# A decoder layer: the attention output turned in 32x32 blocks on VectorE and moved by DMA, in place of TensorE's turn

## The reference

```
q, k, v = x @ Wq, x @ Wk, x @ Wv          # 16 heads of 128
q, k    = rmsnorm(q, q_rms_w), rmsnorm(k, k_rms_w)
scores  = q k^T / sqrt(128) - alibi slope * distance, causal
y       = rmsnorm(softmax(scores) v, subln_w)       # per head, over its 128 columns
x       = layernorm(x + y @ Wproj)                  # y: 1024 x 2048, Wproj: 2048 x 256
x       = layernorm(x + x mixed by softmax(query key^T), query and key from ctx)
x       = layernorm(x + quantised feed-forward(x))  # ternary weights, 8-bit activations
```

## Time and profile before

| | |
|---|---|
| median of 3 runs | 435.72 us (434.96 to 436.02) |
| span of the profiled execution, first to last instruction | 432.9 us |
| time of that execution apart from its span | not given; the median of the runs lies 2.82 us above the span |
| TensorE matmul busy | 401.9 us (93%) |
| VectorE busy | 327.7 us (76%) |
| ScalarE busy | 254.4 us (59%) |
| GpSimd busy | 220.2 us (51%) |
| mean granted TensorE clock | 0.979 |
| DMA | 14.52 MB, 21747 packets |

### The profile page before, as it was taken

One profiled execution on the slowest core, in us unless ns is written; L12 is line 12 of the kernel. 1 busy time (PEld: TensorE's weight loads), 2 busy tenths in 40 slices (PEclk: granted clock), 3 DMA queues, 4 the chain that ended last, 5 costly groups with the idle time before them and its releaser, 6 DMA issues.

```text
span 432.9 us, 9595 instructions
## 1 busy us (share of the span) xinstructions
PE 401.9 (93%) x2605; PEld 361.1 (83%) x2612; DVE 327.7 (76%) x1000; ACT 254.4 (59%) x750; POOL 220.2 (51%) x368
## 2 busy tenths in 40 slices
PE   4979999999999999999999999999999899999552
PEld 3668899999999999999999999999988677777321
DVE  0777987887797798788779779878822788888862
ACT  3486777677676776767767677676722333333321
POOL 3633667676675776767767677675501122222210
PEclk9999999999999999999999999999999999999965
DMA  8980010110101101011010110000000000000000
GB/s 223 316 251 2 2 36 3 38 37 0 36 0 36 36 0 36 0 36 36 0 36 0 36 36 0 0 0 0 0 2 0 2 0 15 12 14 12 13 14 24
DMA packets 21747, 14.52 MB, mean 34 GB/s; under 512 B 1760, under 2 KB 21472, under 8 KB 21728
## 3 DMA queue, kind: packets, MB, share of 16 engines
q1 hardware_dynamic: 21728, 14.29, 11.2%
HBM read 13.24 MB, written 1.05 MB: 33 GB/s over the span
## 4 chain that ended last, share of the span: by engine, by line
PE 86%; DVE 5%; ACT 4%; issue 2%; DMA 1%; POOL 1%; SPq 0%; POOLq 0%; DVEq 0%
PE ps L482 30%; PE ps L422 11%; PE ps L493 7%; PE ps L506 6%; PE ps L499 5%; PE ps L512 4%; PE ps L505 3%; PE ps L514 3%; PE ps L513 3%; PE ps L521 3%; PE ps L587 3%; PE ps L572 2%; ACT hT L696 2%; DMA x_sb<-in_x 1%; PE ps L557 1%
## 5 line engine op out<-in xcount | busy, mean ns | idle before, releaser
L315 POOL TENSOR_TENSOR qk_rstd<-qk_sum,minus_half 128x2 f32<-128x2 f32 x128 | 88.5, 692 | 92.6 <-DVE qk_sum L797 90.8
L482 PE MATMUL ps<-w_hi,xT_hi 128*128 128x384 f32 x256 | 96.9, 378 | 2.3 <-DVE qk_n L791 1.4
L482 PE MATMUL ps<-w_hi,xT_lo 128*128 128x384 f32 x256 | 86.5, 338 | 0.0
L482 PE MATMUL ps<-w_lo,xT_hi 128*128 128x384 f32 x256 | 86.3, 337 | 0.0
L797 DVE TENSOR_REDUCE qk_sum<-sq 128x2 f32<-128x258 f32 x128 | 53.6, 419 | 30.8 <-ACT sq L635 29.1
L635 ACT ACTIVATE sq<-ps 128x256 f32<-128x256 f32 x128 | 49.1, 384 | 34.6 <-PE ps L482 34.4
L791 DVE TENSOR_TENSOR qk_n<-ps,qk_rstd 128x256 f32<-128x256 f32 x128 | 54.2, 423 | 18.8 <-POOL qk_rstd L315 17.8
L422 PE MATMUL ps<-wp,yT 128*128 128x256 f32 x256 | 62.2, 382 | 0.0
L310 POOL TENSOR_TENSOR y_rstd<-y_sum,minus_half 128x2 f32<-128x2 f32 x64 | 49.0, 766 | 24.6 <-DVE y_sum L804 20.9
L673 ACT ACTIVATE sqy<-ps 128x258 f32<-128x258 f32 x64 | 24.8, 387 | 58.5 <-PE ps L514 58.5
L422 PEld LDWEIGHTS ps<-wp,yT 128*128 128x128 f32 x256 | 46.7, 190 | 5.9
(11 more groups left out here) (126 smaller groups left out, 846.9 us busy)
## 6 DMA issues: line engine op xcount, KB each, us to landing
w_raw<-in_L_attn_Wq SPq DMA_DIRECT2D x16, 128.0 KB, 2.2
w_raw<-in_L_attn_Wk SPq DMA_DIRECT2D x16, 128.0 KB, 2.3
w_raw<-in_L_attn_Wv SPq DMA_DIRECT2D x16, 128.0 KB, 2.3
wp<-in_L_attn_Wproj SPq DMA_DIRECT2D x1, 2048.0 KB, 16.1
ff_raw<-in_L_ffn_w_gate SPq DMA_DIRECT2D x1, 1024.0 KB, 8.6
ff_raw<-in_L_ffn_w_up SPq DMA_DIRECT2D x1, 1024.0 KB, 11.0
ff_raw<-in_L_ffn_w_down SPq DMA_DIRECT2D x1, 1024.0 KB, 13.0
out<-fin SPq DMA_DIRECT2D x8, 128.0 KB, 1.7
```

What stands on the lines that cost most here:

```text
L315: pool.tensor_tensor(qk_rstd[:, t, :], qk_sum[:, t, :], minus_half[:], ALU.pow).then_inc(s_rs[t], 1)
L482: last = pe.matmul(ps[:, t, 0:3 * D], xa[:, k, tok], wa[:, r, k * 3 * D:(k + 1) * 3 * D], start=(i == 0), stop=(i == len(parts) - 1))
```

## The change

VectorE turns y_n itself, in 32x32 blocks: an operation `turn_y` behind pT in the step writes all 4 x 4 blocks of both tiles, each turned, to a new buffer `y_blk`. A block is then on the wrong partitions still, except on the diagonal; SyncE moves the blocks by DMAs within SBUF into `yT`, 16 for each head, each 32 partitions by 1 KB. `y_blk` has two halves, for even and odd heads. Within `yT` a head's columns are now ordered so that the eight token tiles lie side by side: a tile's 128 columns have a stride of 8 elements (32 bytes), and the projection's stationary operand is read so. The last three steps (`LATE`) are still turned by TensorE and copied by ScalarE, after the DMAs of their head have landed.

`sub_scale` is no longer applied with the copy but multiplied into `wp`, in four operations on VectorE at the ends of steps 4 to 7. The early projections take 14 heads; heads 14 and 15 of the first two tiles follow behind the drain. Several small buffers of the last stage now lie in `y_blk`.

```diff
+            def move_y(h, r):
+                for db in range(4):
+                    for tb in range(4):
+                        sp.dma_start(yT_cols[db * Q:(db + 1) * Q, bass.ds(h * (B * T) + tb * Q * NT, Q * NT)],
+                                     y_blk[tb * Q:(tb + 1) * Q, r, db].rearrange("p q u -> p (q u)")
+                                     ).then_inc(s_ydma[r], 16)
...
+            with sp.Fori(2, TRIPS) as trip:
                 for r in range(2):
                     sp.wait_ge(s_split, trip * (2 * SPLITS) + SPLITS * (r - 1))
                     load_w(trip * 2 + r, r)
+                    sp.wait_ge(s_blk, trip * PAIR + (r - 3) * B)
+                    move_y(trip * 2 + (r - 4), r)
+            for h in range(H - 4, H):
+                sp.wait_ge(s_blk, h * B + (B if h < H - 1 else B - LATE))
+                move_y(h, h % 2)
...
-                    last = pe.matmul(ps[:, u % 2, 0:C], yT[:, h * B + b, t * P:(t + 1) * P], wp[:, h, :],
+                    last = pe.matmul(ps[:, u % 2, 0:C], yT_parts[:, h, :, u], wp[:, h, :],
...
-                if live(3):
+                if live(3) and isinstance(n, int) and n - 3 >= STEPS - LATE:
                     pe.wait_ge(s_yn, n - 2)
-                    wait(pe, s_yT, n - 3)
+                    wait(pe, s_yT, n - 3 - (STEPS - LATE))
                     for t in range(TT):
                         last = pe.transpose(ps_yT[:, t * P:(t + 1) * P], y_n[:, t, :], ident[:])
...
+            for u in range(TT):
+                project(u, [H - 2, H - 1])
...
-                if live(4):
-                    act.wait_ge(s_ty, n - 3)
-                    act.activation(yT[:, n - 4, :], ps_yT, ACT.Copy, scale=sub_scale).then_inc(s_yT, 1)
+                if isinstance(n, int) and n - 4 >= STEPS - LATE:
+                    act.wait_ge(s_ty, n - 3 - (STEPS - LATE))
+                    act.wait_ge(s_ydma[1], 256 * TRIPS)
+                    own = (n - 4) % B * TT
+                    act.copy(yT_parts[:, H - 1, :, own:own + TT].rearrange("p w t -> p t w"),
+                             ps_yT.rearrange("p (t w) -> p t w", t=TT)).then_inc(s_yT, 1)
...
+            def turn_y(n, j, trip):
+                r, b = j // B, j % B
+                dve.wait_ge(s_yn, n - 2)
+                if b == 0:
+                    wait(dve, s_ydma[r], trip * 256)
+                dve.transpose(y_blk[:, r, :, :, b * TT:(b + 1) * TT].rearrange("p g q t -> p t g q"),
+                              y_n[:].rearrange("p t (g q) -> p t g q", g=4)).then_inc(s_blk, 1)
+
+            def scale_wp(part):
+                dve.wait_ge(s_wp, 16)
+                dve.wait_ge(s_vecs, 3)
+                rows = wp[:, part * 4:(part + 1) * 4].rearrange("p h c -> p (h c)")
+                dve.tensor_scalar(rows, rows, sub_scale, None, ALU.mult).then_inc(s_wps, 1)
...
                     dve.tensor_copy(pT[:], ps_pT).then_inc(s_pT, 1)
+                if live(3) and not (isinstance(n, int) and n - 3 >= STEPS - LATE):
+                    turn_y(n, (j - 3) % PAIR, trip)
                 if live(0):
                     norm(0, n)
...
+                if isinstance(n, int) and B <= n < PAIR:
+                    scale_wp(n - B)
```

More of the change, by code:

```diff
@@ L55, in decoder_kernel @@
     TRIPS = H // 2
-    EARLY = -(-TT * H // 6)
+    Q = P // 4
+    LATE = 3
+    EARLY = -(-TT * (H - 2) // 6)
     CROSS_STEP = 3
@@ L83, in decoder_kernel @@
         yT = sb("yT", [P, STEPS, T])
+        y_blk = sb("y_blk", [P, 2, 4, Q, NT])
         ident = sb("ident", [P, P])
@@ L135, in decoder_kernel @@
         x2 = sb("x2", [P, 2, C])
-        fin = sb("fin", [P, 2, C])
-        x1T = sb("x1T", [P, KC, P])
+        spare_f32 = y_blk[:, 1].rearrange("p g q u -> p (g q u)")
+        fin = spare_f32[:, 0:2 * C].rearrange("p (a c) -> p a c", a=2)
+        x1T = spare_f32[:, 2 * C:3 * C].rearrange("p (k t) -> p k t", k=KC)
+        x_round = spare_f32[:, 3 * C:4 * C]
         x_most, x_scale, x_inv, h_most, h_scale, h_inv, down_scale = (sb(n, [P, 1]) for n in (
@@ L146, in decoder_kernel @@
         sig, hid, h_round = ff_raw[:, 0, 0:F], ff_raw[:, 0, F:2 * F], ff_raw[:, 1, 0:F]
-        hq = sb("hq", [P, F], BF16)
-        hT = sb("hT", [P, FC, P], BF16)
+        spare = y_blk[:, 0].rearrange("p g q u -> p (g q u)").bitcast(BF16)
+        hq = spare[:, 0:F]
+        hT = spare[:, F:2 * F].rearrange("p (f t) -> p f t", f=FC)
         ps = ctx.enter_context(nc.psum_tensor("ps", [P, 8, BANK], F32))
@@ L157, in decoder_kernel @@
         ps_yT = ps[:, 6, 0:T]
+        yT_cols = yT[:].rearrange("p n t -> p (n t)")
+        yT_parts = yT_cols.rearrange("p (h w u) -> p h w u", h=H, u=NT)
         s_x = [sem("x_batch0_loaded"), sem("x_other_batches_loaded")]
@@ L184, in decoder_kernel @@
             "pT_copied", "y_done", "y_squared", "y_summed", "y_normed", "y_turned", "yT_copied"))
+        s_blk = sem("y_blocks_turned")
+        s_ydma = [sem("y_even_head_moved"), sem("y_odd_head_moved")]
+        s_wps = sem("wp_scaled")
         s_mv = [sem(f"mean_var{i}_done") for i in range(3)]
@@ L245, in _ @@
             sp.dma_start(wp[:], wproj.rearrange("(h p) c -> p h c", p=P)).then_inc(s_wp, 16)
-            with sp.Fori(1, TRIPS) as trip:
+            def move_y(h, r):
[4 more added lines that the diff above has]
+                                     ).then_inc(s_ydma[r], 16)
+            for r in range(2):
+                sp.wait_ge(s_split, 2 * SPLITS + SPLITS * (r - 1))
+                load_w(2 + r, r)
+            with sp.Fori(2, TRIPS) as trip:
                 for r in range(2):
@@ L415, in project @@
                         if u < 2:
-                            pe.wait_ge(s_wp, 16)
+                            pe.wait_ge(s_wps, 4)
                             pe.wait_ge(s_qkn[u], STEPS)
+                            pe.wait_ge(s_ydma[0], 256 * (TRIPS - 1))
+                            pe.wait_ge(s_ydma[1], 256 * (TRIPS - 1))
                         else:
                             pe.wait_ge(s_mv[0], u - 1)
-                    if h in (0, H - 1):
-                        pe.wait_ge(s_yT, h * B + b + 1)
-                    last = pe.matmul(ps[:, u % 2, 0:C], yT[:, h * B + b, t * P:(t + 1) * P], wp[:, h, :],
+                    if h == H - 2 and u == 0:
+                        pe.wait_ge(s_ydma[0], 256 * TRIPS)
+                    if h == H - 1 and u == 0:
+                        pe.wait_ge(s_ydma[1], 256 * TRIPS)
+                    if h == H - 1 and b > B - LATE - 1 and t == 0:
+                        pe.wait_ge(s_yT, b - (B - LATE) + 1)
+                    last = pe.matmul(ps[:, u % 2, 0:C], yT_parts[:, h, :, u], wp[:, h, :],
                                      start=(h == 0), stop=(h == H - 1))
@@ L427, in project_early @@
             def project_early(part):
-                for i in range(part * EARLY, min((part + 1) * EARLY, TT * H)):
-                    project(i // H, [i % H])
+                for i in range(part * EARLY, min((part + 1) * EARLY, TT * (H - 2))):
+                    project(i // (H - 2), [i % (H - 2)])
             def beside(n):
@@ L547, in _ @@
                     if m == 0:
-                        pe.wait_ge(s_yT, STEPS)
+                        pe.wait_ge(s_yT, LATE)
                     for k in range(KC):
@@ L689, in _ @@
                     act.wait_ge(s_t1, m + 1)
-                    act.copy(x1T[:].rearrange("p k t -> p (k t)"), ps[:, 2, 0:C]).then_inc(s_x1T, 1)
+                    act.copy(x1T.rearrange("p k t -> p (k t)"), ps[:, 2, 0:C]).then_inc(s_x1T, 1)
                 if m > 0:
@@ L695, in _ @@
                     act.wait_ge(s_th, u + 1)
-                    act.copy(hT[:].rearrange("p f t -> p (f t)"), ps[:, 2, :].bitcast(BF16)).then_inc(s_hT, 1)
+                    act.copy(hT.rearrange("p f t -> p (f t)"), ps[:, 2, :].bitcast(BF16)).then_inc(s_hT, 1)
                 if m < NT:
@@ L810, in step @@
                     dve.wait_ge(s_ry, n - 2)
-                    wait(dve, s_ty, n - 3)
+                    if isinstance(n, int) and n - 3 > STEPS - LATE:
+                        dve.wait_ge(s_ty, n - 3 - (STEPS - LATE))
                     dve.tensor_tensor(y_n[:], ps_y[:, :, 0:D], y_rstd[:].unsqueeze(2).to_broadcast([P, TT, D]),
@@ L894, in _ @@
                     dve.wait_ge(s_hr, u + 1)
-                    dve.tensor_scalar(hq[:], h_round, ROUND + 127.0, -ROUND, ALU.min, ALU.add).then_inc(s_hq, 1)
+                    dve.tensor_scalar(hq, h_round, ROUND + 127.0, -ROUND, ALU.min, ALU.add).then_inc(s_hq, 1)
                 if m > 1:
@@ L901, in _ @@
                     link(act_scale(x_most[:], x_scale[:], x_inv[:]))
[L902 to L903 removed]
+                    link(dve.tensor_scalar(x_round, x2[:, m % 2], x_inv[:], ROUND, ALU.mult, ALU.add))
+                    dve.tensor_scalar(xq[:], x_round, ROUND + 127.0, -ROUND, ALU.min, ALU.add).then_inc(s_xq, 1)
                     dve.tensor_scalar(gate_up_scale[:], w_scale[:, 0:2], x_scale[:], None, ALU.mult).then_inc(s_gus, 1)
```

1 line of the change is left out of this document (removed).

## The result

The changed kernel takes 462.36 us (median, 461.27 to 463.19) against 435.34 in the same series: slower, ratio 1.061 (95% interval 1.059 to 1.064). The forecast was 451, so the sign held, and the size fell short by 11: 462 lies above the band that the forecast gave itself (443 to 460) and inside its wide range (440 to 468). The span of the profiled execution went from 432.9 to 460.2, +27.3 us, where the sum said +15.1.

The account below looks back on a forecast made before the run. The prediction took TensorE as the bound, with a VectorE-GpSimd ring close behind. Loop 10.8, first-trip turns 1.65, scaling 2.0 and moves 0.7 made +15.1 us, a span of 448.0 and a median of 451 (443 to 460; wide range 440 to 468).

Parts of the forecast that it names:

- the sum: Whole kernel: loop 10.8, first trip's turns 1.65, scaling 2.0 and final moves 0.7 add 15.1 us to the profiled span.
- the turn in the ring: Loop, VectorE between pT and tile 0's norm: the turn adds 0.42 us, lengthening seven trips by 10.8 us.
- the ring: Each step: VectorE's norms, sums and copies, then GpSimd's power, which releases the next qk_n; 4.67 us when quantising.
- TensorE is the bound by a few tenths: Loop: TensorE sets plain steps at 4.42 us, with 0.34 us of room before it would wait for qk_n.
- the removal: TensorE's two turns per step go in 61 of 64 steps, 0.23 us a pair, at most 14.0 us.
- The double turn of the rivals: VectorE's turn takes twice per column for its stride, 0.69 us, giving 467 us; chance 0.22.
- The first trip: Before the loop: the turn in five steps adds 1.65 us, the four Wproj scalings on VectorE 2.0 us.
- Strided weight loads at nothing: Projections: reading yT at a 32-byte stride costs nothing, since the 0.11 us load may double under a 0.24 pass.
- The rival on it: Projections: strided weight loads take three times 0.11 us, adding 25 us over 256 passes, giving 476; chance 0.08.
- the prediction's own signs of being wrong: Wrong if TensorE stays without idle time in the loop, or if the passes after the loop lengthen.
- The moves at the end, 0.7: Drain: 32 DMAs for heads 14 and 15 land 17 us after step 59's turn, costing 0 to 2 us, taken as 0.7.
- The hidden turn of the other side: Loop: the turn falls wholly into VectorE's gaps and TensorE stays the bound, giving 424 us; chance 0.15.

Follow-up runs that it names:

- e7: The changed kernel without the call of turn_y, SyncE moving zeros; 442.55 us, 1.016 of the kernel before.
- e4: The changed kernel with the same strided turn put behind the scores, last in VectorE's step; 451.90 us, 1.040 of the kernel before.
- e5: The kernel before with VectorE's turn added behind pT, nothing taken out and nothing reading the turned blocks; 448.26 us, 1.029 of the kernel before.
- e3: The changed kernel with the turn writing 256 contiguous columns instead of columns 32 bytes apart; 454.43 us, 1.044 of the kernel before.
- e2: The changed kernel with the projection reading 128 contiguous columns of yT instead of strided ones; 458.77 us, 1.056 of the kernel before.
- e1: The changed kernel with heads 14 and 15 moved in four DMAs each instead of sixteen; 456.43 us, 1.050 of the kernel before.
- e8: The changed kernel with dense turn and read, the turn at two other places, head 15 kept on TensorE, head 14's passes last; 431.82 us, 0.992 of the kernel before.

## Why the prediction was right in sign and short in size

It was right in sign by its own mechanism, the turn in the ring. That 462 still falls into the wide range is partly luck: the range reached up to 468 for a turn of twice the price, which did not come; the drain and the strided loads, priced at 0.7 and 0, filled its place with 12.1.

- **TensorE is the bound by a few tenths, the ring stands close behind.** Right. e7 takes TensorE's work away and puts no turn in its place: four steps of a trip fall to between 4.20 and 4.29, close to the forecast 4.19 of TensorE's own work, which runs back to back there, and the three with quantising stay at 4.66 to 4.76, the ring's (the eighth, behind these, at about 4.39). That is what the removal is worth, 5.3 us of 14.0.
- **The turn in the ring.** The mechanism was right (e4, e5), the term mis-sized: the turn holds the next norm for 0.48, not 0.42. With 0.48 the forecast's sums give 4.47, 4.68 and 5.06, a trip of 38.16; measured were about 4.45, 4.66 and 5.01 to 5.10, 38.02. So the loop cost 12.8, not 10.8. Dense it would have been 0.36 (e3), below my 0.42, because a turn does overlap its neighbours, which I had denied it: it lasts 0.43 and the next operation starts after 0.36. What I priced from dense rows came out above it through the stride.
- **The double turn of the rivals.** Its cause was there, its price not: 0.63 busy against 0.43 dense, 0.48 against 0.36 start to start. By the Trainium skill (Advanced Engine Details and Errata, SBUF Cachelines), an access that goes to another 16-byte line each time is penalised. e2 and e3 agree in sign, and the penalty here is 1.3 to 1.5 times for the turn and 333 / 196 = 1.7 times for the weight load.
- **The first trip.** Too high by 1.3: the four scalings cost 1.30 (I took 2.0) and the five turns 0.98 (1.65), so part of each was hidden in that trip; where, I didn't follow.
- **Strided weight loads at nothing.** Wrong: 0.033 us a pass in a row, 3.3 us in the last stage (e2). "It may double under its cover" bounded the load against the pass of 0.24, by a row of a turn (0.11), which is a quarter of four matmuls on the chain and not a load (the page of before has 140 ns for those loads), and not by the projection's own load of 190 ns, which that page had too and which fills most of a pass, not a third; a load of 333 ns is longer than the pass. The rival on it had the mechanism and 25 us for it, against 3.3 in the last stage. Longer passes stood among the prediction's own signs of being wrong.
- **The moves at the end, 0.7.** This is the step that failed most: 8.85. Four terms of it were off. An issue took 0.64, not the 0.47 of a load. So the last block landed 343.56 - 321.66 = 21.9 us after the turn of step 59, not 17. And ScalarE stood at its copy already 13.5 us after it (343.56 - 8.37 - 321.66), where I had counted on about 17. The wait was 8.4 us, and with the lower clock behind it the passes took 2.1 more (e1). And the projections of heads 14 and 15, said only to change places, became the last thing that the first residual waits for, 3.34 us in e1, part of the remaining 2.4. I had followed the queue to its landing and stopped there, without timing the one who waits.
- **The hidden turn of the other side.** e8 shows that it can be had, by another place and a dense layout; but its price of 14.0 was the removal at face value, and with the turn wholly hidden it was 5.9 in the loop.

What stays open: which of the two new places in e8 brings more, how much of its gain is the place and how much the dense turn, and how the 2.4 us at the end of e1's drain divide between the late place of the projections and their stride; none of these was run alone.

## What to carry to other kernels

Work taken off the engine that bounds is worth only the distance to the ring behind it; read that distance step by step before pricing the removal. Work added to a second engine costs by its place in that engine's order: between a value and the engine that waits for it, it cost most of what it lasts (0.32 of 0.48 us a step here); in the time in which the engine itself waits, a third of that (e4), and dense and at the two places of e8 nothing. Where a change gives a layout a stride, price every reader and writer of it, and where it leaves a row of DMAs at the end of a loop, time the one who waits for the last.

## What the runs showed of the hardware

- The block turn of 128x256 f32 on VectorE took 0.43 us with columns in a row and 0.63 to 0.69 with each 32 bytes from the last; the weight load of 128 f32 columns took 190 to 196 ns dense and 333 at that stride.
- Sixteen DMAs between parts of SBUF with runs of 128 bytes cost SyncE 10.41 us (e8) and landed in 1.9 us (median); with 1 KB runs 32 cost 20.58 and landed in 1.8. Eight times the runs (87027 packets in the whole of e8, 34035 in the changed kernel) changed neither by much:

```profile
303.62 10.41 SPq L265 DMA_DIRECT2D yT<-y_blk  x16
```

- 4.04 us without work on TensorE were followed by a mean granted clock of 0.67 over 7.24 us of full work; in e1, without the wait, it stayed at 1.00.
